# A token-embedding, attention and expert kernel on one core: gathers of tokens placed between the first attention items, and the routing tables built in pieces

## The reference

```python
h = jnp.take(W.T, x, axis=0)                    # W: 256 x 50257, one column per token
h = h + attn(_layernorm(h))                     # 6 layers
h = h + ffn(_layernorm(h))                      # 8 experts, top 2, and one shared expert
# a layer of attn, for each sequence:
hn = _layernorm(x) * gamma[l] + beta[l]
q, k, v = split(hn @ w_qkv[l]); q = softmax(q, axis=1); k = softmax(k, axis=2)
context = einsum('bic,bjc->bij', k, v)
x = einsum('bic,bij->bjc', q, context) @ w_out[l] + b_out[l] + x
# ffn:
gate = x @ gate_w; top_v, top_i = top_k(gate, 2)
out = sum_e swiglu_e(x) * w_e + swiglu_shared(x)
```

## Time and profile before

| what | value |
|---|---|
| median of three runs | 1444.95 us |
| the profiled execution: time | 1447.14 us |
| its span, first to last instruction | 1445.4 us |
| mean granted TensorE clock, share of full speed | 0.947 |
| busy: PE, DVE, ACT, POOL | 1262.4, 1046.6, 830.8, 959.4 us |
| building the table of embeddings | 0 to 82 us |
| gathers, statistics, first item's preparation | 82 to 146 us |
| attention items | 146 to 974 us |
| feed-forward stage, shared expert and routing | 966 to 1121 us |
| 39 pairs of expert work | 1118 to 1432 us |

### The profile page before, as it was taken

The page is one execution under the profiler, slowest core; times in us unless marked ns, Lnnn a source line. Parts: engine busy times, 40 slices in busy tenths (PEclk is TensorE's granted clock), DMA queues, the critical chain, the costliest instruction groups (busy, mean ns, idle before and its releaser), DMA issues. The chain is left out here.

```text
span 1445.4 us, 37041 instructions
## 1 busy us (share of the span) xinstructions
PE 1262.4 (87%) x10992; PEld 1054.0 (73%) x10993; DVE 1046.6 (72%) x2675; ACT 830.8 (57%) x2286; POOL 959.4 (66%) x958
## 2 busy tenths in 40 slices
PE   4400499999999999999999999988998999999996
PEld 3400388888888888888888888854564888888885
DVE  3246789998898899889989989866765455545553
ACT  2230278878777877888788777767552232332321
POOL 0057889889888888898898889836752143343433
PEclk8755799999999999999999999998999999999998
DMA  9994264543464345335433445654444344544441
GB/s 318 384 319 133 53 117 95 131 111 67 87 134 81 58 110 133 62 68 138 98 65 58 94 109 89 104 85 108 140 123 148 58 65 61 73 62 68 63 64 14
DMA packets 354415, 157.13 MB, mean 109 GB/s; under 512 B 283953, under 2 KB 338737, under 8 KB 354353
## 3 DMA queue, kind: packets, MB, share of 16 engines
q1 hardware_dynamic: 321090, 117.99, 36.0%
q0 software_dynamic: 20064, 25.32, 9.9%
q10 hardware_dynamic: 13200, 13.11, 2.6%
HBM read 44.50 MB, written 42.64 MB: 60 GB/s over the span
## 5 line engine op out<-in xcount | busy, mean ns | idle before, releaser
L731 PE MATMUL bank<-hT,Wc 128*128 128x256 f16 x2304 | 285.9, 275 | 88.3 <-DMA hT<-hhl 76.1
L731 PEld LDWEIGHTS bank<-hT,Wc 128*128 128x128 f16 x2304 | 226.3, 98 | 116.7 <-issue 88.7
L691 POOL DMA_INDIRECT out_rows<-h0b,payin x78 | 121.9, 1562 | 209.7 <-DVE h0b L1471 150.3
L828 PE MATMUL bank<-xTg,Wall 128*128 128x256 f16 x1872 | 211.0, 273 | 0.0
L828 PEld LDWEIGHTS bank<-xTg,Wall 128*128 x1872 | 182.6, 98 | 22.4 <-issue 0.8
L596 POOL TENSOR_TENSOR h0b<-h0b,rows 128x512 f32<-128x512 f32 x96 | 121.8, 1269 | 98.7 <-issue 53.3
L1096 ACT ACTIVATE silu<-bank 128x512 f32<-128x512 f32 x110 | 65.5, 596 | 176.4 <-PE bank L828 150.6
L1399 DVE SCALAR_TENSOR_TENSOR gT<-bank,silu 128x512 f32<-128x512 f32 x110 | 76.0, 691 | 111.4 <-ACT silu L1096 110.6
L731 PE MATMUL bank<-Wc,MT 128*128 128x256 f16 x1152 | 143.8, 275 | 9.2 <-DVE MT L1262 9.2
L731 PE MATMUL bank<-khl,eqT 128*128 128x256 f16 x1152 | 142.0, 273 | 5.7
L731 PE MATMUL bank<-Wc,hT 128*128 128x256 f16 x1152 | 143.1, 275 | 0.0
(11 more groups left out here) (150 smaller groups left out, 2591.6 us busy)
## 6 DMA issues: line engine op xcount, KB each, us to landing
Wall<-in_L_tok_W SPq DMA_DIRECT2D x25, 512.0 KB, 7.8
emb_rows<-Wall ACTq DMA_DIRECT2D x25, 512.0 KB, 11.4
Wall<-in_L_ffn_ew SPq DMA_DIRECT2D x24, 512.0 KB, 4.0
Wc<-Wn SPq DMA_DIRECT2D x48, 128.0 KB, 2.3
Wst<-in_L_attn_w_qkv SPq DMA_DIRECT2D x12, 384.0 KB, 3.6
h_rows<-Wall SPq DMA_DIRECT2D x4, 1024.0 KB, 4.8
X<-h_rows POOLq DMA_DIRECT2D x8, 512.0 KB, 6.7
out_rows<-X SPq DMA_DIRECT2D x8, 512.0 KB
```

Source lines behind the costliest of these rows:

```text
L691: pool.indirect_dma_start(out=out_rows, out_offset=bass.IndirectOffsetOnAxis(ap=got(j % PAYS, w, 0, i32), axis=0), in_=yout[j % 2][:, w, : ...
L731: last = mm(to, lhs(a, k, o), moving, start=(i == 0 and k == 0), stop=(i == 2 and k == 1))
L828: last = mm(to, cols(a, e, 2 * k + w, (2 * half + c) * P, P), moving, start=(n_ == 0), stop=(n_ == 5))
```

## The change

There are four edits.

**Gathers.** Of the 25 chunks the first 5 go to a table `emb_near`, the last 20 to `emb_last`. While the last 20 are built, GpSimd gathers all 32 tiles from `emb_near` (an id outside it fetches nothing); ids below 2560 are then set out of range. After the last store only item 0's two tiles are gathered from `emb_last` (`gather_item`), and the other items' gathers stand between GpSimd's work of the turns, eight turns ahead. Nothing is computed for all of G at once any more: for layer 0 the statistics of item t+7 are taken from G directly, one power gives the roots of both layer norms (of h, and of the normalised h, from the variance), `norm` writes the doubly normalised tile, and `first_x` derives X with b_out added. ScalarE makes the upper half of layer 0's items (`s_hh`). VectorE and GpSimd begin the turns one turn earlier, ScalarE three. Layer 0's weights are cut between the stores of the second step. The loads of expert 0 and 1, of layer 1's weights, and the store of h (8 pieces in place of 4) are moved on SP into layer 0's and 1's turns.

**Pieces beside the items.** Layer 0's CUT turns are 3 to 10 and it has no EXPERT turns. In layers 1 to 3 all 16 turns carry an expert piece, the first 8 of them beside the CUT. Layer 4 has only CUT in its first half. The LAST turns are two turns earlier.

**The last turns and the tables.** The statistics of groups 0 to 3 are spread over the last 8 turns, two tiles each (before: groups 0 to 5 over the last 6, four tiles each); groups 4 and 5 follow in the routing stage. The ScalarE passes of groups 0, 1 and 2 stand in the last 6 turns, one pass each. `tables` is cut into eight functions that stand between the shared expert's pieces of groups 6 and 7.

**The end.** The last pair's two halves go to two matmul banks and are weighed and scattered apart; the product of the pair before it is put before the second half of the last pair's `up`.

```diff
-    XEARLY = NB // 2
-    STRETCH = 5
-    VROWS = STRETCH * VSTEP
+    VLAST = 4
+    VROWS = VLAST * VSTEP
+    FAR = 1 << 20
+    assert -(-VOCAB // VCH) % VBUF == VBUF - 1
...
+    emb_near = nc.dram_tensor("emb_near", (VSTEP, D), f32, kind="Internal").ap()
...
+        def passes(eng):
+
+            eng.wait_ge(s_idmax, 2)
+            past_last = eng.value_load(idover[0:1, 0:1], min_val=0, max_val=VOCAB - 1 - VLAST * VSTEP)
+            return eng.snap(past_last // VSTEP + 1)
 
         def steps(eng):
-            return eng.snap(stretches(eng) * STRETCH)
...
+            for t in range(-lead, HEAD if other else 2):
+                one(t, t % 2, CUT if FIRST_CUT <= t < FIRST_CUT + WSL else PLAIN, None)
...
+                with eng.Fori(HEAD // 2, half) as h:
+                    pair(h, PLAIN)
+                with eng.Fori(1, 4) as l:
+                    with eng.Fori(0, quarter) as b:
+                        pair(eng.snap(l * half + b), CUT, eng.snap((l - 1) * half + b))
+                    with eng.Fori(quarter, half) as b:
+                        pair(eng.snap(l * half + b), PLAIN, eng.snap((l - 1) * half + b))
+                with eng.Fori(4 * half, 4 * half + quarter) as h:
...
-            for e in range(2):
-                load_expert(e)
-            for j in range(4):
-                install(0, j)
-            stage(1)
-            for g in range(4):
-                sp.wait_ge(s_gath[g], (n // STRETCH) * (16 * NT // 4))
-                at = slice(g * NT // 4, (g + 1) * NT // 4)
-                sp.dma_start(h0_rows.rearrange("(t p) d -> p t d", p=P)[:, at, :], G[:, at, :]).then_inc(s_h0st[g], 16)
+
+            def store_h0(h):
...
+                    if l == 0 and i < 1:
+                        stage(1, i + 2)
+                        if i == 0:
+                            stage_rows(1)
+                    if l == 0 and i in (1, 2, 3, 4, 5, 6, 7, 9):
+                        store_h0((i - 1) if i < 8 else 7)
+                    if l == 0 and i in (8, 10, 12):
+                        load_expert(0, (i - 8) // 2)
+                    if l == 1 and i < 1:
+                        load_expert(1, i + 2)
+                    if l in (1, 2) and 2 <= i < 11:
+                        load_expert(3 * l - 1 + (i - 2) // 3, (i - 2) % 3)
...
+                for t in range(NT):
+                    gather(t, idx, emb_near, s_gath[t % 4])
+                pool.tensor_scalar(far[:, :], idx[:, :], VSTEP, FAR, ALU.is_lt, ALU.mult)
+                pool.tensor_scalar(idx_in[:, :], idx[:, :], -VSTEP, None, ALU.add).then_inc(s_far, 1)
+                pool.wait_ge(s_far, q * 3 + 2)
+                pool.sem_inc(s_passed, 1)
+                pool.tensor_tensor(idx_in[:, :], idx_in[:, :], far[:, :], ALU.add).then_inc(s_far, 1)
+                pool.wait_ge(s_far, q * 3 + 3)
                 pool.sem_inc(s_passed, 1)
...
+            def gather_item(i):
+
+                if i >= 4:
+                    pool.wait_ge(s_item[i % 4], 16 * TB * (i // 4))
+                for t in range(TB * i, TB * (i + 1)):
+                    gather(t, idx_in, emb_last, s_item[i % 4])
...
+                if early(t + 4) and t >= 0:
+                    pool.wait_ge(s_hh, t + 5)
+                    low_half(t + 4, p)
+                if early(u):
+                    pool.wait_ge(s_rows, 48)
+                    pool.wait_ge(s_xb, u + 1)
+                    pool.tensor_tensor(xn[:, :, :], xn[:, :, :], row(0), ALU.mult).then_inc(s_hg, 1)
+                    pool.wait_ge(s_hg, u + 1)
+                    if u >= 1:
+                        pool.wait_ge(s_h, u)
+                    pool.tensor_tensor(hf[:, :, :], xn[:, :, :], row(1), ALU.add).then_inc(s_hf, 1)
+                    if t + 8 < NB:
+                        gather_item(t + 8)
+                    if t < -1:
+                        pool.wait_ge(s_hh, u + 1)
+                        low_half(u, 1 - p)
+                elif have(u):
...
+                if early(w) and t == w - 7:
+                    pool.wait_ge(s_amv, w + 1)
+                    if w >= 2:
+                        pool.wait_ge(s_xb, w - 1)
+                    pool.tensor_scalar(evar[1 - p][:, TB:], amv[1 - p][:, :, 1], EPS, None, ALU.add)
+                    pool.tensor_scalar(evar[1 - p][:, 0:TB], amv[1 - p][:, :, 1], 1.0 + EPS, EPS * EPS, ALU.mult, ALU.add).then_inc(s_avar, 1)
+                    pool.wait_ge(s_avar, w + 1)
+                    pool.tensor_tensor(erstd[1 - p][:, :], evar[1 - p][:, :], mhalf[:, 0:2 * TB], ALU.pow).then_inc(s_arstd, 1)
...
+                    elif end:
...
+            with act.Fori(0, m) as step:
+                act.wait_ge(s_reuse, step + 1)
+                for j in range(VBUF):
+                    chunk(step, j, emb_near, j * VCH)
+            for f_ in range(VLAST):
+                step = act.snap(m + f_)
+                for j in range(VBUF):
+                    r0 = act.snap(first_column(act, step, j) - m * VSTEP).with_bounds(
+                        min_val=0, max_val=VROWS - VCH, guaranteed_mod_val=0, out_of_modulus=1)
+                    if f_ == VLAST - 1 and j >= VBUF - 2:
+                        act.wait_ge(s_fill, 17)
+                    chunk(step, j, emb_last, VROWS - VCH if f_ == VLAST - 1 and j == VBUF - 1 else r0)
+                    if f_ == 0:
+                        for n_ in range(2 * j, min(2 * j + 2, WSL)):
+                            cut(n_, 0, n_)
 
...
+                i = t + 5 if isinstance(t, int) and t < -1 else t + 4
+                if early(i) and t != -1:
+                    act.wait_ge(s_hf, i + 1)
+                    if i >= 2:
+                        act.wait_ge(s_hT[i % 2], landed(i - 2))
+                    A(hhl[i % 2][:, 0, :, :], hf[:, :, :], ACT.Copy).then_inc(s_hh, 1)
...
+            item_loop(act, one, 5, between={
+                **{ITEMS - 6 + 2 * g: partial(normed, g) for g in range(3)}, **{ITEMS - 5 + 2 * g: partial(high, g) for g in range(3)}})
...
+                if early(w):
+                    for k in range(TB):
+                        last = V.scalar_tensor_tensor(eratio[:, k:k + 1], evar[p][:, k:k + 1], erstd[p][:, k:k + 1],
+                                                      erstd[p][:, TB + k:TB + k + 1], ALU.mult, ALU.mult)
+                    last.then_inc(s_quot, 1)
+                    for k in range(TB):
+                        last = V.tensor_scalar(xn[:, k, :], G[:, w * TB + k, :], amv[p][:, k, 0:1], erstd[p][:, k:k + 1],
+                                               ALU.subtract, ALU.mult)
+                    last.then_inc(s_xn, 1)
+                    return
...
+            def first_x(w, p):
+
+                dve.wait_ge(s_rows, 48)
+                dve.wait_ge(s_quot, w + 1)
+                dve.wait_ge(s_xn, w + 1)
+                for k in range(TB):
+                    last = V.scalar_tensor_tensor(X[:, w * TB + k, :], xn[:, k, :], eratio[:, k:k + 1], rows[:, 0, 2, :],
+                                                  ALU.mult, ALU.add)
+                last.then_inc(s_xb, 1)
...
+                if early(t + 5):
+                    first_x(t + 5, 1 - p)
...
+                **{ITEMS - 8 + i: partial(stats_of, i // 2, 2 * (i % 2), 2 * (i % 2) + 2) for i in range(8)}})
...
+                if g == NG - 1:
+                    pair_bases(ends)
+                    pair_experts()
...
-                if g + 1 == NG - 1:
-                    tables()
+                if g == NG - 2:
+                    counts()
+                if g == NG - 1:
+                    pair_starts()
                 gate_shared(g, 2)
+                if g == NG - 2:
+                    pair_counts()
+                if g == NG - 1:
+                    pair_places()
+                    pair_words()
                 gate_shared(g, 3)
+                if g == NG - 2:
+                    ends = pair_ends()
 
...
+            gate(SHP + PAIRS - 1, 0)
+            weigh(PAIRS - 2, 1, (PAIRS - 2) % PAYS, (PAIRS - 2) // PAYS + 1)
+            gate(SHP + PAIRS - 1, 1)
```

362 lines of the change are left out of this document (195 added, 167 removed).

## The result

The changed kernel takes **1422.34 us** (median of 4 runs, 1420.69 to 1423.30) where the kernel before, measured beside it, takes 1444.63: a ratio of 0.9845 [0.9828, 0.9862]. The forecast was 1398, range 1382 to 1415: right in sign, wrong by 24 us. The profiled execution took 1423.30 with a span of 1421.4. Measured again four times later, on two chips, it took 0.9998, 0.9998, 1.0016 and 0.9861 of the kernel before, so the gain of 22 us is not there at all times. In the three bad ones the table of embeddings ends some 20 us later, which is taken up with the experiments. The kernel before was 6 to 10 us slower at those times too (medians 1450.89, 1450.96 and 1454.96 us), which the ratios take out.

What follows compares the result with a forecast made beforehand. Memory traffic bounds the table, a chain of 32 gathers the 64 us hole, TensorE the turns, VectorE and GpSimd close. Terms -55.3 + 6.2 + 4 + 3.6 - 0.6 - 2.8 - 0.8 - 1.5 = -47.2: median 1398, range 1382 to 1415.

Steps and rivals of the forecast that it cites:

- PR of item 0: Start of layer 0: paced by GpSimd's beta of item 4, it comes at 129.0 us, 55.3 earlier than 184.3.
- The first product: Start, TensorE: with few gathers ahead of item 0, first product at 103.5 us, 42.7 earlier, before the table's share.
- The turns with gathers: Items 0 to 9: 8.9 us a turn instead of 8.21, giving back 6.2 us, between -2 and +22.
- Rival A: Turns with gathers: GpSimd holds VectorE up, 10.7 us a turn instead of 8.9, 16 us more, 1414; chance 0.15.
- SP waits in them for nothing late, so nothing is charged: Turns of layers 0 and 1: expert loads, layer 1's weights and the store of h move there at no cost.
- The table: Building the embedding table: near gathers and fill add traffic, +4 us, range up to +15.
- Rival B: Cuts or near gathers stretch the table by 13, or double pieces cost 0.5 a turn: 1407 and 1406; chance 0.15.
- Pieces in layers 1 to 3: Turns with cut and expert piece: 0.15 us more in each of 24, +3.6, up to +16; layer 4 -0.6.
- The end of the turns: After item 95: groups 0 to 2 done early, so transposes are early and waits go; -2.8 us.
- The tables and the end: Routing tables: old stall goes, a wait for the first pair's load comes, net -0.8; last scatters wait less, -1.5.
- Rival C: Routing stage: late stalls do go, first pair's load hidden, no waits before group 2; 7 + 8 less, 1383; chance 0.17.
- Rival D: GpSimd, turns -5 to 7: the 26 gathers between items starve, at 3.6 us each 1457; chance 0.02.

Runs made afterwards that it cites:

- Experiment 2: Changed kernel with ScalarE copying item 3's upper half behind item 0's exponentials instead of ahead of them: 1418.31 us, 0.9810 of the kernel before.
- experiment 6: Changed kernel with layer 1's eight weight cuts in turns 8 to 11, two each, instead of one each in turns 3 to 10: 1465.58 us, 15.0 more than its control.
- experiment 12: Changed kernel with three unused 128x32 GpSimd instructions added in each of turns 0 to 7: 1459.81 us, 2.8 more than its control.
- experiment 3: Changed kernel with the three broadcast loads of layer 1's gamma, beta and b_out issued in turn 9 instead of turn 0: 1423.66 us, 0.9844 of the kernel before.
- experiment 11: Changed kernel with SP issuing group 0's four transposes ahead of the last item's turn instead of behind all turns: 1453.74 us, 3.3 less than its control.
- experiments 1: Changed kernel with GpSimd's scatters of group 0 ahead of the root of group 5 instead of behind it: 1420.82 us, 0.9822 of the kernel before.
- Experiments 9: Changed kernel with group 0's scatters ahead of group 5's root and group 4's statistics ahead of the last item's addition: 1444.49 us, 5.9 under its control.
- experiment 4: Changed kernel with the pieces ending in `pair_at` right behind the experts' piece in the last group: 1416.27 us, 0.9792 of the kernel before.
- experiment 14: Changed kernel with the 32 near gathers begun only when all stores of both tables have landed: 1464.92 us, its control 1425.51.
- experiment 8: Changed kernel without the near table, its gathers and the fill, one table of five steps instead: 1429.01 us, 21.4 less than its control.

## Why the prediction was wrong, step by step

Forecast were -47.2 us, measured -23.9. Of the 23.3 between them 8.5 lie ahead of PR of item 0, 6.2 in the turns with gathers, 9.5 in the last turns and the routing stage, 1.5 in the table, 1.3 in the tables and the end; 3.7 came back in the layers between. So three terms failed: the start, the pace of the turns, and the end of the turns.

- **The first product: right.** Forecast 42.7 us earlier without the table, 103.5 + 4 = 107.5; measured 108.94, 1.5 of it the table.
- **PR of item 0: the step that failed in the start.** The sum let GpSimd's beta of item 4 pace it ("PR of item 0 at 129.0", 133 with the table) and never followed ScalarE, to which the change gave the upper halves, and which runs in order. It came at 142.95 on VectorE, 8.4 us later than forecast when the table's 5.5 are added to it (134.5). Experiment 2 took 4.6 of them back by ScalarE's order alone; the other 3.8 were not taken apart.
- **The turns with gathers: right mechanism, 0.62 too small.** 8.9 forecast, 9.52 measured, inside the bounds. Missing in GpSimd's sum of 8.5 are 0.33 for the roots (1.83 us from start to start, 1.5 estimated), 0.28 for gamma and beta (2.78 from start to start, 2.5 estimated), 0.18 for the lower half beside `first_x`, and the wait of 0.43 for VectorE. Rival A had the pair of `first_x` right (2.28 us), but the two normalisations, of which its price of 0.60 each was read, were not stretched (0.72 for both). That GpSimd's work counts for the pace is shown by experiments 6 and 12.
- **"SP waits in them for nothing late, so nothing is charged": wrong.** The loads moved into the turns did not make SP wait, but a gather: 3.05 us, 12.68 in the step. What its removal is worth, 0 to 3 us, experiment 3 does not settle.
- **The table: +5.5 against +4 in the profile compared, right, and in part by luck.** In three of the four later measurements the first gather out of `emb_last` started at 107 to 111 us, beyond the 93 that the forecast gave as a sign of being wrong. Rival B had the place, near gathers that stretch the table, with 13 us; that they can cost over 20 lay outside the bound of +15, and no row of before could have shown it.
- **Pieces in layers 1 to 3: the first halves right** (layer 2: 8.41 us a turn, forecast about 8.4; before 8.28; +3.1 in the 24 turns against +3.6). But other turns became shorter, which the forecast did not follow: the second halves of layers 1 to 3 by 1.6 us together, though they keep their piece, both halves of layer 4 by 1.8 against a forecast of 0.6, and items 9 to 16 by 0.8, where layer 0 lost its pieces. So +3.0 became -0.7; why those with a piece became shorter was not taken apart.
- **The end of the turns: wrong in sign.** The forecast argued with which waits go, and held the transposes to be early because their group was. SP issues them behind all turns, so TensorE waited 2.95 us (experiment 11). And it did not follow GpSimd's new order: the root of group 5, whose statistics had been moved behind rank 1, stands ahead of the scatters of group 0, for which ScalarE's group 4 waits (experiments 1 and 9). Experiments 9 and 11 took 5.9 and 3.3 us back, about the 9.5 by which this term was off.
- **The tables and the end: right.** Wait of 5.22 forecast 4.5, low clock 2.52 forecast 2.4, net 0.0 forecast -0.8; end -1.0 forecast -1.5. Rival C (the late stalls go) fell; it takes experiment 4's edit to get its 7.7.
- **Rival D: a slip.** 1409 + 50 is 1459; the 1457 given are the forecast's 1398 and 26 gathers of 2.26 us more, 59. Nothing came of D here: gathers took 1.0 to 1.15 us busy in the turns.
- **VectorE beside GpSimd.** Beside GpSimd's work `first_x`, which reads two tiles, took 2.28 us instead of 0.87, GpSimd's lower half 1.33 instead of 1.15. VectorE pays most of it; the gathers of these turns took 0.99 to 1.15 us busy, no more than before. The page SBUF — State Buffer of the Trainium skill (section "Who interferes with whom") says that a VectorE instruction with two inputs in SBUF contends with a GpSimd instruction that reads SBUF; the trace agrees with it for `first_x`. No run shows what the page says of GpSimd's descriptors.

## What to carry to other kernels

When work moves from one in-order engine to another, follow the receiving engine's program line by line: a copy put ahead of an exponential waits for its producer, and everything behind it too. Statistics or loads that are spread out to fill gaps turn into what someone waits for as soon as a scatter or a gather stands behind them, so look for the consumer's queue and not only for the gap. And GpSimd gathers beside a stage that keeps all DMA engines busy are a risk that one profile may not show: measure at several times, always with a control beside it.

## What the runs showed of the hardware

Gathers of GpSimd issued while the stores and loads of the table filled the DMA engines cost 3.8 us at some times (87.94 - 84.11, experiment 14) and over 20 in others (107.29 - 82.87, experiment 8), on the same chips with the same program; in the bad ones the mean share of the engines fell to 0.08 in stretches. In the changed kernel's profile the 12 matmuls of 128x512 behind a wait of TensorE took 4.45 us after 0.91, 4.12 after 2.05 and 4.54 after 6.79 us of waiting, at a mean granted clock of 0.62, 0.66 and 0.60 of 2.4 GHz, but 2.76 after 2.95 and after 0.84 us, at 1.00: the length of the wait alone doesn't say what the clock costs behind it.
